# Pairwise products of 32 fields: one transfer for tile 0, other loads, and a list of 72 store slots that repeats by halves

## The reference, cut to what matters

```python
def reference(x, W):                       # x: [4096, 32, 64] f32, W: [64, 64] f32
    vid = jnp.einsum('bfd,de->bfe', x, W)
    i, j = jnp.triu_indices(32, k=1)       # 496 pairs of fields
    return x[:, i, :] * vid[:, j, :]       # [4096, 496, 64] f32
```

## Time and profile before

| | before |
|---|---|
| median of 3 runs | 1284.44 us (1284.42 to 1284.62) |
| span of the profiled execution | 1282.9 us |
| VectorE busy | 1079.9 us (84%) |
| TensorE busy | 184.4 us (14%) |
| moved by DMA | 553.70 MB, 432 GB/s over the span |
| transfers | 82: 8 loads, 74 stores |

### The profile page before, as it was taken

One profiled execution on the slowest core, in us unless ns is written; L12 is line 12 of the kernel. 1 busy time (PEld: TensorE's weight loads), 2 busy tenths in 40 slices (PEclk: granted clock), 3 DMA queues, 4 the chain that ended last, 5 costly groups with the idle time before them and its releaser, 6 DMA issues. The chain is left out here.

```text
span 1282.9 us, 1255 instructions
## 1 busy us (share of the span) xinstructions
PE 184.4 (14%) x256; PEld 71.9 (6%) x256; DVE 1079.9 (84%) x273; POOL 0.2 (0%) x4
## 2 busy tenths in 40 slices
PE   2012110302111030300020211103020030202100
PEld 1000000100000010100010000001010010100000
DVE  6589989988897989998028989989998899899980
POOL 0000000000000000000000000000000000000000
PEclk7555565655655565655565565656565565655655
DMA  9999999999999999999999999999999999999999
GB/s 406 424 427 438 435 433 435 443 431 427 437 438 433 425 437 434 436 429 445 418 419 427 436 430 436 438 438 424 440 439 429 432 435 439 425 439 439 431 423 409
DMA packets 11810, 553.70 MB, mean 432 GB/s; under 512 B 1312, under 2 KB 1312, under 8 KB 1312
## 3 DMA queue, kind: packets, MB, share of 16 engines
q1 hardware_dynamic: 6048, 277.38, 50.1%
q10 hardware_dynamic: 5760, 276.30, 49.9%
HBM read 33.59 MB, written 520.09 MB: 432 GB/s over the span
## 5 line engine op out<-in xcount | busy, mean ns | idle before, releaser
L295 DVE TENSOR_TENSOR mem<-mem,vid 128x1024 f32<-128x1024 f32 (+11 forms) x270 | 1079.3, 4065 | 161.5 <-DMA out_dram<-mem 113.2
L315 PE MATMUL vid<-mem,w 128*128 x256 | 184.4, 888 | 1010.2 <-PEq L313 1010.2
L315 PEld LDWEIGHTS vid<-mem,w 128*128 128x128 f32 x256 | 71.9, 295 | 1121.9 <-issue 1121.9
L226 DVE COPY w<-mem 64x64 f32<-64x64 f32 x2 | 0.4, 189 | 5.0 <-DMA mem<-in_r_x_dram 4.9
L223 DVE MEMSET w<- 128x128 f32 x1 | 0.2, 165 | 0.8 <-PEq L340 0.8
L340 POOL MEMSET const-bfloat16-1.0<- 128x1 bf16 x1 | 0.1, 102 | 0.0
L340 POOL MEMSET const-uint8-127<- 128x1 uint8 x1 | 0.1, 102 | 0.0
L340 POOL MEMSET const-float32-0.0<- 128x1 f32 x1 | 0.1, 98 | 0.2 <-issue 0.2
L340 POOL MEMSET const-float32-1.0<- 128x1 f32 x1 | 0.1, 98 | 0.0
## 6 DMA issues: line engine op xcount, KB each, us to landing
out_dram<-mem SPq DMA_DIRECT2D x9, 7680.0 KB, 23.3
out_dram<-mem ACTq DMA_DIRECT2D x3, 7680.0 KB, 23.1
out_dram<-mem SPq DMA_DIRECT2D x3, 7168.0 KB, 21.6
out_dram<-mem ACTq DMA_DIRECT2D x3, 5120.0 KB, 17.5
out_dram<-mem ACTq DMA_DIRECT2D x2, 7168.0 KB, 22.6
out_dram<-mem ACTq DMA_DIRECT2D x2, 6656.0 KB, 21.4
out_dram<-mem SPq DMA_DIRECT2D x2, 6656.0 KB, 19.8
out_dram<-mem ACTq DMA_DIRECT2D x3, 4096.0 KB, 17.5
```

What stands on the lines that cost most here:

```text
L226: lambda: nc.vector.tensor_copy(w2[half, half], mem[half, place + F, :D]),
L295: lambda: nc.vector.tensor_tensor(o, left, right, ALU.mult),
L315: last = nc.tensor.matmul(vid[:, b : b + BANK, :], lhsT=w2[:, :], rhs=xt(b), start=True, stop=True)
```

## The change

Tile 0 and W come in one transfer. `load(0)` has two pieces; `load(1)` has three others, tile 8 alone, then tiles 9 to 12, then 13 to 15. The slot list is new, 36 slots for eight tiles, used twice, so that slot 35 ends with tile 7 and slot 36 begins with tile 8. The wait of a group's first store for a load is gone. In its place `HELD_UNTIL` lets the first store of each half wait for a later product: slot 0 goes out after pair 184 of the first half, slot 36 after pair 168 of the second. There are 78 transfers: 6 loads and 72 stores.

```diff
 GROUPS = [
-    (0, [(96, 224), (26, 96), (0, 26)]),
-    (8, [(154, 256), (26, 154), (0, 26)]),
+    (0, [(96, 224), (0, 96)]),
+    (8, [(224, 256), (96, 224), (0, 96)]),
 ]
-STRETCHES = [37]
-SLOTS = [
-    (80, 256), (109, 336), (83, 240, 16), (56, 323, 13), (64, 379), (80, 240), (56, 323), (64, 379),
...
+HALF_RUN = [
+    (96, 256), (92, 352), (60, 240), (68, 300, 52), (76, 368), (100, 240), (104, 340, 28), (68, 224), (80, 292, 48),
+    (72, 372), (104, 236), (104, 340, 32), (124, 192, 44), (128, 316, 24), (124, 176, 16), (120, 300, 16), (88, 160),
+    (96, 252, 48), (96, 348), (128, 188), (128, 316), (128, 164), (128, 296, 20), (128, 144, 20), (128, 276, 20),
+    (128, 120), (128, 256, 20), (128, 88), (128, 232), (128, 72), (128, 200, 32), (128, 48, 24), (128, 176, 24),
+    (128, 316), (128, 48), (120, 268, 48),
 ]
+SLOTS = HALF_RUN * 2
+STRETCHES = [len(HALF_RUN)]
+HELD_UNTIL = {0: 184, len(HALF_RUN): 168}
...
-BREAKS = sorted({a + s for a, (_, _, *seams) in zip(STARTS, SLOTS) for s in seams} | set(STARTS))
+BREAKS = sorted(
+    {a + s for a, (_, _, *seams) in zip(STARTS, SLOTS) for s in seams}
+    | set(STARTS)
+    | {STARTS[slot] + pairs for slot, pairs in HELD_UNTIL.items()}
+)
...
-    first = [
-        transfer(
-            mem[:, :, :].rearrange("p u c -> p (u c)")[:, (place + HALF) * C : (place + F) * C + D],
-            x0.rearrange("p u c -> p (u c)")[:, HALF * C : F * C + D],
-            (place + HALF, place + F + 1), False, [],
-        ),
-        transfer(mem[:, place : place + HALF, :], x0[:, :HALF, :], (place, place + HALF), False, []),
-    ]
+    first = transfer(
+        mem[:, :, :].rearrange("p u c -> p (u c)")[:, place * C : (place + F) * C + D],
+        x0.rearrange("p u c -> p (u c)")[:, : F * C + D],
+        (place, place + F + 1), False, [],
+    )
...
-        if hold:
-            needs.append((hold[-2], 16))
-            hold = []
...
-            hold = load(begins.index(t))
-            for late in held:
-                store(*late)
-            held = []
+            load(begins.index(t))
...
-            if at == end:
-                late = (slot, counts[made])
-                group = sum(behind <= slot for behind in STRETCHES)
-                if t < begins[group]:
-                    held.append(late)
-                else:
-                    store(*late)
+            for late, pairs_made in HELD_UNTIL.items():
+                if at == STARTS[late] + pairs_made:
+                    store(late, counts[made])
+            if at == end and slot not in HELD_UNTIL:
+                store(slot, counts[made])
```

More of the change, by code:

```diff
@@ L226, in pairwise_bilinear_kernel @@
             lambda: nc.vector.tensor_copy(w2[half, half], mem[half, place + F, :D]),
-            [(place + F, place + F + 1)], [(first[0], 16), (made, 1)], made,
+            [(place + F, place + F + 1)], [(first, 16), (made, 1)], made,
         )
-    nc.vector.wait_ge(made, 3).then_inc(free, 1)
-    nc.vector.wait_ge(first[1], 16).then_inc(free, 1)
+    nc.vector.wait_ge(made, 3).then_inc(free, 2)
     owed = 0
-    loads = [(range(1), (place, place + F + 1), sem) for sem in first]
+    loads = [(range(1), (place, place + F + 1), first)]
     def load(g):
@@ L238, in load @@
         low = place_of(end - 1, F)
-        sems = []
         for lo, hi in pieces:
             at = (begin - 1) * F + lo - low
-            sems.append(transfer(mem[:, lo:hi, :], x[:, at : at + hi - lo, :], (lo, hi), False, after((lo, hi)), act if g else sp))
-            loads.append((range(begin, end), (lo, hi), sems[-1]))
-        return sems
+            queue = act if g else sp
+            sem = transfer(mem[:, lo:hi, :], x[:, at : at + hi - lo, :], (lo, hi), False, after((lo, hi)), queue)
+            loads.append((range(begin, end), (lo, hi), sem))
     def loaded(t):
@@ L248, in loaded @@
         return [(sem, 16) for tiles, piece, sem in loads if t in tiles and overlap(piece, units)]
-    hold = load(0)
+    load(0)
     begins = [begin for begin, _ in GROUPS]
-    held = []
     def store(slot, last):
-        nonlocal hold
         begin, end = STARTS[slot : slot + 2]
```

## The result

| | before | changed |
|---|---|---|
| median | 1284.43 us (4 runs) | 1296.40 us (4 runs, 1296.08 to 1296.66) |
| ratio | | 1.0093, 95% interval 1.0078 to 1.0107 |
| span of the profiled execution | 1282.9 us | 1295.4 us |
| transfers | 82 | 78 |

The changed kernel is 12.0 us (0.93%) slower. The forecast was 1292.9 in a range of 1291.0 to 1295.2: the sign and the gap at the seam came true, the size was 3.5 us short, and the time lies above the range. In the span, 1295.35 against a forecast 1291.4, it is 3.9 us: the forecast added the 1.50 us that lay between median and profiled span before, and here they are 1.05 apart.

What follows compares the result with a forecast made beforehand. The prediction took the always-full DMA queue, at 435 GB/s, as the bound. Span 1282.94 + 8.5 - 0.0 = 1291.4, plus 1.50 between span and median, gave 1292.9 us, range 1291.0 to 1295.2.

Steps and rivals of the forecast that it cites:

- The seam: Between the halves: tile 8's first product waits for tile 9's load, the queue empties, and the kernel is 8.5 us behind.
- 3872 units remain in both, at the same rate: After both seams, old and new kernel have equally many 64 KB units left, so the remainder costs nothing extra.
- The head: First store held until pair 184: its overlap with the loads shrinks from 1.5 to about 0.3 us, gaining 1.2.
- Fewer transfers: Whole kernel: 82 transfers become 78, each costing 0.02 to 0.03 us in a full queue; a gain of 0.1 us.
- The one transfer for tile 0: At the start: tile 0 and W land together at 8.25, 2.4 us later; only the first store waits for it.
- The turn: Between the halves, going from stores to loads loses 1.1 us; for the range, nothing or twice that.
- The new list: Slots after the seams: the tightest store leaves 3.8 us before the queue would run dry, so it costs nothing.
- Rival B: A store needs over 3.8 us to get going, so the six tightest slots add gaps too: 1303 us; 3 in 100.
- Rival C: Every transfer has a fixed price that returns when it goes: 1285 us, same as before; 1 in 100.
- Rival A: At the seam, tile 8's first product doesn't wait for tile 9, so no stall: 1282.9 us; 9 in 100.

Runs made afterwards that it cites:

- experiment 1: Changed kernel, but tile 8's first product no longer asks for tile 9's load; median 1285.54 us, ratio to before 1.0010.
- experiment 2: Changed kernel, with slot 36 stored after pair 96 of the second half instead of 168; median 1286.63 us.
- experiment 3: Kernel before with its own slot list and loads, but slots 0 and 1 stored after pair 200; median 1285.54 us, ratio 1.0011.
- the control: The kernel before, unchanged, profiled again beside the others; median 1284.25 us.
- experiment 4: Experiment 1 with the first store leaving after pair 152 instead of 184; median 1284.95 us, ratio 1.0004.
- experiment 6: Experiment 1 with slots 36 and 37 both held until pair 200; median 1287.44 us (a first version, holding only slot 36, 1297.66).

## Why the prediction was wrong in size

- **The seam: right.** The `free` that a slot's end pushes to the next tile, and the wait for tile 9 that comes with it, did what the part on the seam says: VectorE idle 53.9 us (forecast 52), ended by a load, SP's store at 692.8 (forecast 690), a dip from 684 to 693. Experiments 1 and 2 take it away from two sides, 10.9 and 9.8 us. The gap was 9.9 us, in the sum 706.5 - 681.7 - 14.5 = 10.3. Its unknown f, what a store on an empty queue takes beyond its data (taken as 2.0, from 1.03 to 2.6), was 16.0 - 14.5 = 1.5.
- **The step that failed** is the sentence "3872 units remain in both, at the same rate", and its like for the first half, which the sum did not even name. The rate was taken from a queue whose stores had begun beside loads. Begun on an empty or nearly empty queue, the same stream loses 2.0 to 2.3 us in a half where before lost 0.3 to 0.7; the changed kernel does so in both halves, 1.7 + 1.6 = 3.3 us more. That is most of the 3.9 us that the span was short; the turn, below, is most of the rest. No row of before showed such a start, and the prediction should have put bounds on the rate behind it, as it did for f. The ends that it names for its range add up to 1290.4 and 1295.8, a little wider than the range it states; 1296.4 lies above both, as the rate is not among them.
- **The head: its size was right by chance.** Forecast 1.2 of gain, measured 1.1; but experiment 3 and the control show that such a gain isn't kept. At the end of the first half before, the control and experiment 3 are together within 0.5 us (slot 36 lands at 642.07, 642.0 and 642.5), whatever the head lost. The lower end of 0 was nearer the right value over the half. The Trainium skill, "DMA: Bandwidth & Descriptors", section "Issuing engines are not separate DMA queues", by which, as the prediction read it, overlap costs nothing, comes out nearer than my reading of the late landing at 43.74; for the overlap itself 0.1 (control) and 1.5 us (before) were measured.
- **Fewer transfers: nothing visible**, as said. The one transfer for tile 0, which the sum gave no cost of its own, brings it 0.5 us later in the mean of the executions; the medians don't show it clearly. The 2.0 us that the prediction quotes from the Trainium skill for each DMA ("DMA: Bandwidth & Descriptors", section "Anatomy of one DMA") are given there for transfers that GpSimd issues; those of this kernel are issued by SP and ACT.
- **The turn** from stores to loads cost 2.2 us against 1.9 with the late third load of before, where the sum held 1.4 (1.1, and 0.3 in the landing of old slot 36): 0.8 short, against 0.4 that the gap was smaller.
- **The new list: right** in that no other slot left a gap. Rivals B and C did not occur. Rival A is experiment 1, without the wait: 1285.5 against the 1282.9 given for it, too low by the same rate and head.

## What stays open

Shown is that the stream's time over half a millisecond goes with how the first store meets the loads (table, and experiments 3, 4 and 6, which change that start), and not with the list or VectorE's stall. The traces also show why engines in step lose 1.0 us once: one of them halts, and no other is far enough behind to hide it. That engines in step slow each other down fits the one that halted, which was faster while it was behind the others and no longer when they had caught up. No run changed the step alone, and the kernel with seven small stores loses as much with its engines spread over 2.0 us; so this remains a reading, and not shown.

## What to carry to other kernels

Where a token is told "by the next instruction that may", follow it across the seam of a stage: it takes its waits along, and a list that fits the stage better can move it onto the wrong load. Where a kernel lives by one full queue, hold nothing back at its start: a store that joins a few microseconds before the loads end cost about a microsecond there (experiment 1: 1.1 us) and saved as much or more over the next half millisecond (2.0 us against experiment 6). Before judging a head or a seam by one execution, look at the landing a stage later.

## What was not expected of the hardware

- The same stream of 3872 pairs took 584.6 to 585.0 us when its first store had joined running loads at least 4 us before their end, and 585.5 to 586.6 when it had started under 2 us before their end or behind it (0.1 to 0.3%).
- Engines that start together stay close: in the changed kernel all 16 still begin the last slot's packets within 0.6 us (1276.3 to 1276.9), nearly 600 us behind their first store. Fifteen small extra stores ahead did not part them (0.6 us), seven did (2.0 us), and the stream was no faster for it.
- A 64 KB packet of a store averages 2418 ns on some engines and 2423 to 2425 ns on others of the same execution, for nearly 200 us, and the landings follow the engine that is last.
- Once in the second half one DMA engine halts for 0.65 to 0.96 us (thirteen executions). The stream loses it only where no other engine is that far behind.
- A first load of 32.5 fields landed at 8.6 to 9.3 us in one piece, and at 8.3 to 8.6 us in two pieces on the same queue.
- A store of 64 pairs on 8 partitions delayed the stream by 4.6 us, where a 32 KB row is some 1.2 us of one engine's time in the full stream (estimated as half of a 64 KB packet's 2.4). Here each of its eight 32 KB packets took 4.8 to 5.6 us.
